# A causal mask in two attention stages: from TensorE's scores to VectorE's maxima

## The chip, the cores and the metric

The kernel runs on one core of one Trainium2 chip. Its time is the device time of one execution in microseconds. Three runs of the kernel before gave a median of 2519.93 us (2519.81 to 2523.47).

## The reference

A network of eight layers on X of shape 16 x 256 x 128 in fp32. Each layer adds its result to x. In order: differential attention, a mixture of experts with GELU, causal attention with 16 heads, the same mixture again, single-head attention, full attention with a SwiGLU mixture, a gated linear recurrence, and the attention and mixture before it once more. Two of the attentions are causal. The second of them, cut to what matters (`L0_attn_b`, per sequence of 256 positions, 16 heads of width 8):

```python
scores = jnp.einsum('bhcd,bhsd->bhcs', qi, k) * scale
mask = kpos[None, :] <= qpos[:, None]
scores = jnp.where(mask, scores, jnp.finfo(scores.dtype).min)
p = jax.nn.softmax(scores, axis=-1)
return (None, jnp.einsum('bhcs,bhsd->bhcd', p, v))
```

The differential attention (`L0_attn_a`) has 8 heads with two score maps of width 16 each, masked in the same way; its output is the first map's minus a weighted second map's, normed over 32 channels.

## The kernel before

The program is a row of stages with barriers between them. One function, `attention_stage`, makes four of them. Stage A1 (`kind` "diff") runs from about 16 to 428 us of the profile, stage A2 ("causal") from about 680 to 995 us; for both `masked` is true. A4 and A5 ("full") are not masked. Between them lie the expert stages (F1 to F4), the single-head stage A3 and the recurrence RR.

The code of each engine is written out by hand and runs in order; the engines meet at semaphores. In a masked stage the work goes in steps `n`. A step is four score maps (a quad) of one sequence, so there are `NQ` = 4 steps for each of 16 sequences. Each step has two halves `h`, each with two maps, `k` = 0, 1 (called `j` on VectorE). Scores are computed twice: once as queries x keys, only to find each query's maximum, and once turned, keys x queries, for the exponential. The kernel before does for each half:

- TensorE, `scores` (L1693): waits for `s_free` (VectorE has read the scores of the half before) and `t_free`, then `mask(k)` for both maps (L1675): a bf16 matmul of an identity (`identb`) with a mask tile (`maskS`, -1e30 above the diagonal, else 0) writes the mask into columns 0:128 and 256:384 of the map's bank. Then `score` (L1681) adds the scores on top. Query tile 0 needs keys 0:128 and lies in columns 0:128 of the map, query tile 1 needs keys 0:256 and lies in columns 128:384, so its diagonal block is columns 256:384. In between and behind, `score_t` (L1689) computes the turned scores of the step two before into `tbank`.
- VectorE, `top` (L1432): a `reduce_max` over [2 maps x 128] for query tile 0 (L1439) and one over [2 maps x 256] for tile 1 (L1440) into `padm`, then `s_free`.
- ScalarE, `exp` (L1254), into `Pm`. GpSimd, `causal` (L1133): an affine select clears what lies above the diagonal in `Pm`. That is a mask of its own, over the turned scores.

For each step TensorE also runs `weigh` (L1716, waits for GpSimd's select), `turn_max` (L1731, turns the maxima of the next step), `turn_back` (L1724) and a share of the projections of the sequence two ahead. VectorE adds the turned maxima into the queries (`with_max`, L1450) and does the statistics, norms, the division by the sums, the difference (A1), and the routing for the next expert stage (L140 to L221), each at a fixed place between two maxima. A stage has 66 steps of `top`, that is 132 halves; the two masked stages have 264. In A1 the operations L1454 to L1478 form a chain with GpSimd (`head_root`, L1091 to L1095), which gives `rr` for L1478. In A2 `dense_low` (L1401) waits for ScalarE's `high` (L1231). GpSimd also issues `send` (L225), the indirect DMAs of the routed rows, between its selects.

GpSimd builds the fp32 mask `mf` in `Pm[0]` at the start of a stage; VectorE casts it into `maskS` and the identity into `identb` (L1422, L1423).

Of the kernel before, what the change touches and what calls it, by code (L numbers as in the profile page):

```python
# [7 lines left out]
BF16 = mybir.dt.bfloat16  # L8
I32 = mybir.dt.int32
U32 = mybir.dt.uint32  # L10
ALU = mybir.AluOpType
ACT = mybir.ActivationFunctionType
AX = mybir.AxisListType.X

P = 128
D = 128
SEQ = 256
# [32 lines left out]
class Stage:  # L50
# [6 lines left out]
    def sb(self, name, shape, dt=F32):  # L57
        return self.ctx.enter_context(self.nc.sbuf_tensor(name, shape, dt))
# [4 lines left out]
    def sem(self, name):  # L63
        s = self.nc.alloc_semaphore(name)
        self.sems.append(s)
        return s
# [807 lines left out]
def attention_stage(nc, tag, kind, G, w):  # L874

    X, Y, ident = G["X"], G.get("Y"), G["ident"]
    diff, full, masked = kind == "diff", kind == "full", kind != "full"
# [10 lines left out]
    PW = 384 if masked else 512  # L888
# [52 lines left out]
    insc, outsc = sb("insc", [P, 1]), sb("outsc", [P, 1])  # L941
    if masked:
        mf = Pm[0][:, :, :].rearrange("p j k -> p (j k)")[:, 0:2 * P].rearrange("p (c k) -> p c k", k=P)
        identb, maskS = sb("identb", [P, P], BF16), sb("maskS", [P, 2, P], BF16)
    sbank, tbank = st.bank(f"{tag}_s", 2), st.bank(f"{tag}_t", 2)
    shared = [st.bank(f"{tag}_misc{k}") for k in range(2)]
    mbank, obank = st.bank(f"{tag}_mt"), st.bank(f"{tag}_ot")
# [46 lines left out]
    NEND = offset(NP, 0)  # L994
    assert NM % 2 == NMR % 2
    tail_bank = [shared[NEND % 2], shared[(NEND + 1) % 2]]
    dense_high = sem("dense_high")

    if diff:
        RSLOT = {(0, 0, 0): ("first_max", "first_gaps"), (0, 0, 1): ("first_ranks", "first_lowest", "first_choice", "others"),  # L1000
# [30 lines left out]
    with st.block() as block:  # L1031
# [334 lines left out]
        def _(dve):  # L1366
# [3 lines left out]
            def stat(b):  # L1370
                if full and b > 2:
                    dve.wait_ge(xhat_ready, b)
                for t in range(TPS):
                    last = dve.bn_stats(stats[:, t, :], XS[:, b + S0, t, :])
                last.then_inc(stat_step, 1)
                dve.wait_ge(stat_step, b + 1)
                dve.memset(spare[:, :], 0.0)
                for t in range(TPS):
                    last = dve.bn_aggr(mv[:, t, :], stats[:, t, :])
                last.then_inc(mv_ready, 1)  # L1380
# [38 lines left out]
            if split:  # L1419
                dense_low(lead["D"], 0, lead_bank["D"])  # L1420
            if masked:
                dve.tensor_copy(identb[:, :], ident[:, :])  # L1422
                dve.tensor_copy(maskS[:, :, :], mf[:, 0:2, :])  # L1423
            for k in range(2):
                dve.memset(V[k][:, :, :, DV:VG], 0.0)
            dve.memset(V[1][:, :, :, 0:DV], 0.0).then_inc(v_step, 1)
# [5 lines left out]
            def top(n, h, r, lead_in=False):  # L1432
                dve.wait_ge(s_psum, n * 2 + h + 1)
                if h == 0 and not lead_in:
                    dve.wait_ge(mt_full, n - 1)
                tops = padm[r][:, :, 2 * h:2 * h + 2, MROW]
                if masked:
                    two = sbank[:, :].rearrange("p (j k) -> p j k", j=2)
                    dve.reduce_max(tops[:, 0, :], two[:, :, 0:P], AX)  # L1439
                    last = dve.reduce_max(tops[:, 1, :], two[:, :, P:PW], AX)  # L1440
                else:
                    last = dve.reduce_max(tops.rearrange("p t j -> p j t"),  # L1442
                                          sbank[:, :].rearrange("p (j t k) -> p j t k", j=2, t=TPS), AX)
                last.then_inc(s_free, 1)
# [70 lines left out]

            dve.wait_ge(misc_full, lead["T"] + 1)
            stat(1)
            for n in range(2):
                for h in range(2):
                    top(n, h, n, lead_in=True)  # L1520
                    if (n, h) == (0, 0):
                        norm(1)
                        if full:
                            norm2(1)
# [104 lines left out]
        def _(pe):  # L1629
# [41 lines left out]
                    last = pe.matmul(misc[:, t * VW:(t + 1) * VW], xT[:, t * P:(t + 1) * P], wv[:, :], start=True, stop=True)  # L1671
                last.then_inc(misc_full, 1)

            def mask(k):
                pe.matmul(sbank[:, k * 512:k * 512 + PW].rearrange("p (c k) -> p c k", k=P)[:, 0::2, :], identb[:, :], maskS[:, :, :], start=True, stop=True)  # L1675

            def score(h, g, q, t):
                c, nk, o = g * SEQ, P if masked and t == 0 else SEQ, P if masked and t else t * SEQ
                for k in range(2):
                    r = slice((2 * h + k) * GR, (2 * h + k + 1) * GR)  # L1680
                    last = pe.matmul(sbank[:, k * 512 + o:k * 512 + o + nk], QS[q][r, c + t * P:c + (t + 1) * P], KS[q][r, c:c + nk],  # L1681
                                     start=not masked, stop=True, skip_group_check=masked)
                return last

            def score_t(h, g, q, t):
# [7 lines left out]
            def scores(n, h, g, q, first=False):  # L1693
                pe.wait_ge(s_free, n * 2 + h + 1)
                if not first:
                    pe.wait_ge(t_free, (n - 2) * 2 + h + 1)
                    if h == 0:
                        pe.wait_ge(mt_read, n)
                if masked:
                    for k in range(2):  # L1700
                        mask(k)
                gs, qs = (g, q) if first else ((g + 2) % NQ, q if g < 2 else 1 - q)
                score(h, gs, qs, 0)
                if not first:
                    score_t(h, g, q, 0)
                score(h, gs, qs, 1).then_inc(s_psum, 1)
                if not first:
                    score_t(h, g, q, 1).then_inc(t_psum, 1)
# [862 lines left out]
```

## Time and profile before

| | us |
|---|---|
| median of three runs | 2519.93 |
| span of the profiled execution | 2522.1 |
| stage A1, about | 16 to 428 |
| stage A2, about | 680 to 995 |
| TensorE busy, whole span | 2226.5 (88%) |
| VectorE busy, whole span | 1726.6 (68%) |

The profiled execution is one more execution of the same program; its span is all that the profile shows of its own time, and it is 2.2 us (0.1%) above the median. The hardware profiler gives each instruction's start and duration. "PEld" is TensorE's weight load, which overlaps the matmuls. A duration covers an instruction from start to finish; the next one on the engine can begin before that, so durations in sequence can add up to more than the busy time. A busy TensorE is not TensorE at its peak.

### The profile page before, as it was taken

The numbers are of one execution on the slowest core, as the hardware profiler recorded it, in microseconds if no ns is written. First come the engines' busy times: TensorE is split into PE (matmuls) and PEld (weight loads), VectorE is DVE, ScalarE is ACT, GpSimd is POOL, SyncE is SP. The second block draws the span as 40 slices with busy tenths as digits, with TensorE's granted clock in tenths as the row PEclk, the third lists the DMA queues.
The fourth block names the chain that finished last, engine by engine and source line by source line (L and its number), as shares of the span: only waits on it lengthen the run. The fifth ranks groups of instructions, "written<-read, shape, count | busy, mean of one in ns | idle before, by whom it ended". The sixth has DMA issues, their size and how long they took to land. (4 is left out here: it accounts for less than half of the span.)

```text
span 2522.1 us, 59734 instructions
## 1 busy us (share of the span) xinstructions
PE 2226.5 (88%) x19192; PEld 1631.9 (65%) x19192; DVE 1726.6 (68%) x4756; ACT 1597.0 (63%) x3564; POOL 1213.1 (48%) x1722
## 2 busy tenths in 40 slices
PE   8999998899699887999779888899698788888996
PEld 5666665699466655799666555589444455555795
DVE  6677776444578786544667888666788577886666
ACT  5666665377466665577548888544476178886444
POOL 4456665455244555455123566456411234665563
PEclk9999999899799999999879999899897989998998
DMA  8100000322300001222200000223300000001225
GB/s 284 63 6 12 13 12 11 102 67 71 80 2 6 16 15 53 79 70 64 71 5 2 9 17 18 71 67 82 97 1 1 5 2 4 17 17 55 67 79 138
DMA packets 134005, 116.57 MB, mean 46 GB/s; under 512 B 22919, under 2 KB 120213, under 8 KB 131664
## 3 DMA queue, kind: packets, MB, share of 16 engines
q1 hardware_dynamic: 116432, 78.17, 11.0%
q0 software_dynamic: 17280, 34.65, 4.2%
q8 instruction: 164, 2.69, 0.5%
q14 instruction: 129, 1.06, 0.1%
HBM read 58.22 MB, written 56.36 MB: 45 GB/s over the span
## 5 line engine op out<-in xcount | busy, mean ns | idle before, releaser
L1254 ACT ACTIVATE A_Pm<-A_t 128x768 f32<-128x768 f32 (+1 forms) x512 | 468.6, 915 | 157.6 <-PE A_t L1689 153.5
L371 POOL DMA_INDIRECT ybuf<-F_yo,F_idx x284 | 315.7, 1112 | 248.9 <-DVE F_yo L580 146.0
L1442 DVE TENSOR_REDUCE A_padm<-A_s 128x4 f32<-128x1024 f32 x264 | 322.7, 1222 | 66.1 <-PE A_s L1681 64.7
L225 POOL DMA_INDIRECT xbuf<-xs,dst x256 | 270.0, 1055 | 104.0 <-issue 58.4
L741 PE MATMUL F_hb<-F_xT,F_wt 128*128 128x128 f32 x2272 | 305.9, 278 | 1.0 <-issue 0.6
L1716 PE MATMUL A_ot<-A_Pm,A_V 128*32 128x256 f32 (+3 forms) x3640 | 296.8, 390 | 11.0 <-POOL A_Pm L1133 10.0
L1689 PE MATMUL A_t<-A_Q,A_K 32*128 32x256 f32 (+1 forms) x2560 | 305.9, 333 | 0.0
L1133 POOL TENSOR_SCALAR_AFFINE_SELECT A_Pm<-A_Pm 128x512 f32<-128x512 f32 x256 | 167.7, 655 | 285.6 <-ACT A_Pm L1254 284.0
L741 PEld LDWEIGHTS F_hb<-F_xT,F_wt 128*128 128x128 f32 x2272 | 275.6, 192 | 7.2 <-issue 2.4
L1681 PE MATMUL A_s<-A_K,A_Q 32*128 32x256 f32 (+1 forms) x1584 | 202.1, 332 | 60.0 <-DVE A_padm L1442 42.1
L753 PE MATMUL F_out<-F_WA,F_g 128*128 x1704 | 244.9, 280 | 6.1 <-DVE F_g L571 3.0
L753 PEld LDWEIGHTS F_out<-F_WA,F_g 128*128 128x128 f32 x1704 | 212.8, 191 | 8.9 <-issue 7.6
L1681 PEld LDWEIGHTS A_s<-A_K,A_Q 32*128 32x128 f32 x1584 | 122.8, 188 | 145.8 <-DVE A_padm L1442 72.0
L590 DVE COPY F_wt<-F_WA 128x644 f32 (+1 forms) x284 | 131.0, 462 | 122.7 <-DVE F_yo L580 72.7
L1689 PEld LDWEIGHTS A_t<-A_Q,A_K 32*128 32x128 f32 x2560 | 203.4, 185 | 6.3
L1716 PEld LDWEIGHTS A_ot<-A_Pm,A_V 128*32 128x32 f32 (+1 forms) x3640 | 114.4, 114 | 122.0 <-issue 50.1
L427 ACT ACTIVATE F_g<-F_hb,F_wt 128x128 f32<-128x128 f32 x568 | 162.1, 368 | 32.9 <-PE F_hb L741 32.8
L1440 DVE TENSOR_REDUCE A_padm<-A_s 128x2 f32<-128x512 f32 x264 | 180.5, 684 | 0.0
L1439 DVE TENSOR_REDUCE A_padm<-A_s 128x2 f32<-128x256 f32 x264 | 112.8, 427 | 85.0 <-PE A_s L1681 83.8
L1258 ACT ACTIVATE A_OT<-A_ot 128x256 f32<-128x256 f32 (+1 forms) x260 | 113.9, 438 | 81.7 <-PE A_ot L1716 81.7
L1724 PE MATMUL A_ot<-ident,A_OT 128*128 128x128 f32 x650 | 128.9, 297 | 2.2 <-ACT A_OT L1258 2.2
L1450 DVE TENSOR_TENSOR A_Q<-A_Q,A_mt 128x256 fp32r<-128x256 f32 (+1 forms) x260 | 108.3, 416 | 31.2 <-PE A_mt L1731 20.0
(424 smaller groups left out, 4938.6 us busy)
## 6 DMA issues: line engine op xcount, KB each, us to landing
F_xr<-xbuf SPq DMA_DIRECT2D x284, 68.0 KB, 1.9
xbuf<-A_zero SPq DMA_DIRECT2D x16, 1088.0 KB, 18.0
xs<-ybuf SPq DMA_DIRECT2D x32, 512.0 KB, 7.0
ybuf<-F_yo,F_idx POOLq DMA_INDIRECT x284, 2.5
xbuf<-xs,dst POOLq DMA_INDIRECT x256, 2.6
F_WA<-in_L_ffn_ew SPq DMA_DIRECT2D x2, 2048.0 KB, 9.2
F_WA<-in_L_ffn_ew SPq DMA_DIRECT2D x16, 256.0 KB, 5.6
F_WA<-in_L_ffn_e_gate SPq DMA_DIRECT2D x2, 1024.0 KB, 5.8
```

The costliest lines, as they stand in the source:

```text
L225: pool.indirect_dma_start(out=G["XBUF"][:, :], out_offset=bass.IndirectOffsetOnAxis(ap=G["dst"][:, t, c:c + 1], axis=0), in_=G["xs"][c][:, ...
L371: pool.indirect_dma_start(out=YBUF[:, :], out_offset=bass.IndirectOffsetOnAxis(ap=idx[n][:, h:h + 1], axis=0), in_=yo[r][:, h, :], in_offs ...
L427: last = act.activation(g[q][:, c, :], hb[2 * q + c // 2][:, c % 2 * TILE:(c % 2 + 1) * TILE], ACT.Gelu_apprx_tanh, bias=b1[r][:, c:c + 1])
L741: pe.matmul(hb[2 * q + c // 2][:, c % 2 * TILE:(c % 2 + 1) * TILE], w1[r][:, c * P:(c + 1) * P], xT[q][:, 0:TILE], start=True, stop=True). ...
L753: last = pe.matmul(outb[:, h * D:(h + 1) * D], g[q][:, c, h * P:(h + 1) * P], w2[:, bass.ds(e, 1), c, :].rearrange("p a d -> p (a d)"), st ...
L1133: pool.affine_select(out=keep, in_=keep, compare_op=ALU.is_ge, fill=0.0, base=0, pattern=[[0, 2], [0, 2], [1, P]], channel_multiplier=-1). ...
L1254: act.activation(Pm[r][:, j:j + 2, :], tbank[:, :].rearrange("p (j k) -> p j k", j=2)[:, :, 0:PW], ACT.Exp, scale=SCALE).then_inc(t_free, 1)
L1440: last = dve.reduce_max(tops[:, 1, :], two[:, :, P:PW], AX)
L1442: last = dve.reduce_max(tops.rearrange("p t j -> p j t"), sbank[:, :].rearrange("p (j t k) -> p j t k", j=2, t=TPS), AX)
L1681: last = pe.matmul(sbank[:, k * 512 + o:k * 512 + o + nk], QS[q][r, c + t * P:c + (t + 1) * P], KS[q][r, c:c + nk], start=not masked, stop ...
L1689: last = pe.matmul(tbank[:, k * 512 + keys(t).start:k * 512 + keys(t).stop], K1[q][r, c + t * P:c + (t + 1) * P], Q2[g % 2][r, q0:SEQ], st ...
L1716: last = pe.matmul(obank[h * VG:(h + 1) * VG, 0:NS * SEQ].rearrange("p (s q) -> p s q", s=NS)[:, :, q0:], V[q][:, s, g * QUAD // NS + h, : ...
```

## The change

The mask is no longer put into PSUM by TensorE. `score` writes plain scores, and `top` adds the mask while it takes the maximum: one `tensor_tensor_reduce` for each map and each query tile, four for a half (two over 128 elements, two over 256). Each reads the scores out of PSUM and an fp32 mask row `mask3` ([128 x 384]: the diagonal block's mask, zeros, the mask again) out of SBUF, writes the sum as bf16 into a tile `masked_s` that nothing reads, and gives the maximum as a second output into `padm`. `identb`, `maskS`, `mask` and its calls are gone. At the start of a stage two casts become a clearing and two copies, with a semaphore `mask_set` that VectorE itself waits for ahead of the first maximum. GpSimd's select on `Pm` stays.

```diff
     if masked:
-        identb, maskS = sb("identb", [P, P], BF16), sb("maskS", [P, 2, P], BF16)
+        mask3, masked_s = sb("mask3", [P, 3 * P]), [sb(f"masked_s{k}", [P, 2, 2, PW], BF16) for k in range(2)]
...
-    dense_high = sem("dense_high")
+    dense_high, mask_set = sem("dense_high"), sem("mask_set")
...
             if masked:
-                dve.tensor_copy(identb[:, :], ident[:, :])
-                dve.tensor_copy(maskS[:, :, :], mf[:, 0:2, :])
+                dve.memset(mask3[:, P:2 * P], 0.0)
+                for c in (0, 2):
+                    last = dve.tensor_copy(mask3[:, c * P:(c + 1) * P], mf[:, 0, :])
+                last.then_inc(mask_set, 1)
...
                 tops = padm[r][:, :, 2 * h:2 * h + 2, MROW]
                 if masked:
-                    two = sbank[:, :].rearrange("p (j k) -> p j k", j=2)
-                    dve.reduce_max(tops[:, 0, :], two[:, :, 0:P], AX)
-                    last = dve.reduce_max(tops[:, 1, :], two[:, :, P:PW], AX)
+                    for j in range(2):
+                        for t, (c, width) in enumerate(((0, P), (P, SEQ))):
+                            last = dve.tensor_tensor_reduce(masked_s[r][:, h, j, c:c + width], sbank[:, j * 512 + c:j * 512 + c + width], mask3[:, c:c + width],
+                                                            1.0, -3e38, ALU.add, ALU.max, tops[:, t, j:j + 1])
...
             stat(1)
+            if masked:
+                dve.wait_ge(mask_set, 1)
...
-            def mask(k):
-                pe.matmul(sbank[:, k * 512:k * 512 + PW].rearrange("p (c k) -> p c k", k=P)[:, 0::2, :], identb[:, :], maskS[:, :, :], start=True, stop=True)
-
             def score(h, g, q, t):
...
-                                     start=not masked, stop=True, skip_group_check=masked)
+                                     start=True, stop=True)
...
-                if masked:
-                    for k in range(2):
-                        mask(k)
                 gs, qs = (g, q) if first else ((g + 2) % NQ, q if g < 2 else 1 - q)
                 score(h, gs, qs, 0)
```

## Rows read from the trace of the kernel before

**Rows 1.** The page: span, and busy time of each engine.
```profile
span 2522.1 us, 59734 instructions
...
PE 2226.5 (88%) x19192; PEld 1631.9 (65%) x19192; DVE 1726.6 (68%) x4756; ACT 1597.0 (63%) x3564; POOL 1213.1 (48%) x1722
```

**Rows 2.** Busy time by stretch: inside A1, then inside A2.
```profile
core 0: us, PE busy (x) PEld busy (x) DVE busy (x) ACT busy (x) POOL busy (x), PEclk, DMA share, GB/s
100.00:400.00 300.00, 300.00 (x2484) 199.13 (x2484) 225.15 (x623) 197.86 (x389) 178.92 (x228) 1.00 0.03 10
750.00:950.00 200.00, 177.57 (x2107) 120.89 (x2107) 161.41 (x518) 135.85 (x275) 106.88 (x168) 1.00 0.04 12
```

**Rows 3.** Groups by line, VectorE, 100 to 400 us: the first maximum.
```profile
L1439 DVE TENSOR_REDUCE A_padm<-A_s 128x2 f32<-128x256 f32 x94 | 39.8, 424 | 31.0 <-PE A_s L1681 30.5
```

**Rows 4.** The same, 750 to 950 us.
```profile
L1440 DVE TENSOR_REDUCE A_padm<-A_s 128x2 f32<-128x512 f32 x85 | 58.0, 682 | 0.0
L1439 DVE TENSOR_REDUCE A_padm<-A_s 128x2 f32<-128x256 f32 x85 | 35.9, 422 | 13.7 <-PE A_s L1681 13.3
```

**Rows 5.** Timeline of TensorE in A2: start, duration, instructions.
```profile
838.12 0.38 PE L1675 MATMUL A_s<-A_maskS,A_identb 128*128 128x256 bf16 x2
838.43 0.33 PE L1681 MATMUL A_s<-A_K,A_Q 32*128 32x128 f32 x2
```

**Rows 6.** Waits over 16 to 428 us (A1): total, times, longest.
```profile
DVE A_padm L1439 <- PE A_s L1681: 52.4, 91, 2.6
...
DVE A_ctx L1478 <- POOL A_rr L1095: 25.5, 16, 1.6
DVE X L1490 <- ACT A_Q L1224: 21.2, 15, 2.0
...
PEld A_s L1675 <- DVE A_padm L1440: 1.7, 3, 0.8
```

**Rows 7.** Waits over 698 to 995 us (A2).
```profile
PEld A_s L1675 <- DVE A_padm L1440: 27.1, 51, 1.0
...
DVE A_low L1401 <- ACT A_high L1231: 14.0, 16, 1.0
PEld A_ot L1716 <- POOL A_Pm L1133: 13.8, 20, 1.2
```

**Rows 8.** Timeline of VectorE in A2, one maximum and what follows.
```profile
819.62 0.42 DVE L1439 TENSOR_REDUCE A_padm<-A_s 128x2 f32<-128x256 f32 x1
819.95 0.68 DVE L1440 TENSOR_REDUCE A_padm<-A_s 128x2 f32<-128x512 f32 x1
820.54 0.41 DVE L1450 TENSOR_TENSOR A_Q<-A_Q,A_mt 128x256 fp32r<-128x256 f32 x1
820.87 0.15 DVE L175 TENSOR_TENSOR d<-A_r 128x4 f32<-128x4 f32 x1
...
821.54 0.43 DVE L1439 TENSOR_REDUCE A_padm<-A_s 128x2 f32<-128x256 f32 x1 [0.35 <-PE A_s L1681]
```

**Rows 9.** Groups by line, whole span: two-operand adds and multiplies out of PSUM.
```profile
L1450 DVE TENSOR_TENSOR A_Q<-A_Q,A_mt 128x256 fp32r<-128x256 f32 x195 | 81.4, 418 | 31.2 <-PE A_mt L1731 20.0
...
L580 DVE TENSOR_TENSOR F_yo<-F_out,F_wt 128x128 f32<-128x128 f32 x142 | 41.4, 291 | 77.0 <-PE F_out L753 76.7
```

**Rows 10.** Timeline of ScalarE: operations that also give a sum.
```profile
1324.74 0.30 ACT L1300 ACTIVATE A_squares_next<-Y 128x128 f32<-128x128 f32 x1
1324.94 0.19 ACT L1300 ACTIVATION_READ_ACCUMULATOR A_squares_next<-Y 128x1 f32 x1
1325.03 0.30 ACT L1300 ACTIVATE A_squares_next<-Y 128x128 f32<-128x128 f32 x1
```

**Rows 11.** Timeline of VectorE: seven clearings of one element.
```profile
5.59 0.23 DVE L1368 MEMSET A_credit<- 128x1 f32 x7 [0.41 <-PEq L813]
```

**Rows 12.** Timeline of VectorE, a multiply beside GpSimd work in A1.
```profile
261.95 1.64 DVE L1460 TENSOR_TENSOR A_T<-A_O,A_rec 128x1024 f32<-128x1024 f32 x1
```

**Rows 13.** The same multiply at the end of A1, GpSimd idle.
```profile
434.83 1.22 DVE L1460 TENSOR_TENSOR A_T<-A_O,A_rec 128x1024 f32<-128x1024 f32 x1
```

## The prediction

> **What bounds the kernel now.** I read the page first: TensorE is busy for 88% of the span and VectorE for 68% [rows 1]. That is an average over ten stages, and the change touches only two of them, so the next view is the busy time by stretch. The reader should see two different cases there. Inside A1 TensorE is busy all the time, VectorE for 225 of 300 us. Inside A2 TensorE leaves a gap (178 of 200 us) and VectorE is busy for 161 us [rows 2]. The groups by line give the number of maxima in these stretches, 94 and 85 [rows 3, 4]. One half of a step, which holds one maximum, therefore takes 300 / 94 = 3.19 us in A1 and 200 / 85 = 2.35 us in A2. VectorE is busy for 225.15 / 94 = 2.40 us and 161.41 / 85 = 1.90 us of that. TensorE needs 3.19 and 2.09 us.
>
> The waits say who holds whom. In A1 TensorE hardly ever waits for a maximum (3 times), while VectorE waits 91 times for scores [rows 6]: TensorE is the bound. In A2 TensorE waits for a maximum in 51 of 132 halves, 27.1 us together, and 20 times for GpSimd's select [rows 7]. There the loop of scores, maximum, scores is already closed in a good part of the halves, and VectorE sits in it.
>
> **What is removed.** In each half TensorE no longer issues the two mask matmuls. Their cost is not their duration of 0.38 us but the step from their start to the first score: 838.43 - 838.12 = 0.31 us [rows 5]. For 132 halves that is 41 us of TensorE in each stage, and for A1, if nothing else came in, 41 us of time. The loop gains too: from the end of one maximum (820.63) to the start of the next (821.54) pass 0.91 us now [rows 8], and 0.60 us without the masks.
>
> **What is added.** Today a maximum takes from 819.62 to 819.95 + 0.68 = 820.63, so 1.01 us [rows 8]. After the change four operations stand there, two over 128 and two over 256 elements, each with two operands, one out of PSUM. The trace has no such operation that also gives a maximum, so I cost it in two parts.
>
> The pass over the elements: the nearest rows are the two-operand operations out of PSUM, 291 ns for 128 and 418 ns for 256 elements, so 127 ns for 128 elements more [rows 9]. On the engine's path an operation counts by its step: 820.54 to 820.87 is 0.33 us for 256 elements [rows 8], hence 0.33 - 0.13 = 0.20 us for 128. Two of each are 1.06 us, and the last one ends 0.09 us after its step (0.418 - 0.33): 1.15 us, 0.14 us more than today. The whole of that comes from paying the fixed part four times in place of two.
>
> Giving out the maximum: the nearest rows are ScalarE's operations that also give a sum. The profile shows a second instruction for it, which starts 0.20 us after its operation, and the next operation starts another 0.09 us later [rows 10]. The lower end is VectorE's own smallest work that only writes, seven one-element clearings in 0.23 us, 0.03 us each [rows 11]. I take 0.07 us, nearer to the read-out, because it is the same kind of work, and below it, because ScalarE's fixed parts are longer throughout. Four times 0.07 is 0.28 us. The Trainium skill (VectorE: DVE Perf Modes, "Two Vector instructions with no wait between them") says of this engine too that an operation that also writes out its accumulator is two instructions. No row of this trace shows it on VectorE. By that rule the 0.28 us are due; were the maximum given for nothing, the sum below would be 54 us faster than before and not 20 us slower.
>
> So a maximum becomes longer by x = 0.14 + 0.28 = 0.42 us, from 1.01 to 1.43.
>
> **The sum by stage.** VectorE's new half is its busy time, plus x, plus the idle time that stays.
> A1: idle time is 3.19 - 2.40 = 0.79 us a half. 52.4 / 132 = 0.40 of that is waiting for scores [rows 6] and goes, since TensorE would now need only 3.19 - 0.31 = 2.88. The waits for GpSimd's `rr` (25.5 / 132 = 0.19) and for ScalarE's copy ahead of `add_y` (21.2 / 132 = 0.16) [rows 6] lie on chains of their own and stay: 0.35. The new half is 2.40 + 0.42 + 0.35 = 3.17 us against 3.19, so -3 us over 132 halves. The bound moves from TensorE to VectorE and the gain is eaten.
> A2: idle time is 0.45 us. The wait for scores, 13.3 / 85 = 0.16 [rows 4], shrinks. The wait for `high` is 14.0 / 132 = 0.11 [rows 7] and stays, and I leave 0.09 for halves in which VectorE has less than 0.60 us of other work to fill the loop: 0.20. The new half is 1.90 + 0.42 + 0.20 = 2.52 us against 2.35, so +0.17, or +22 us.
> Together +20 us, worked out against the profiled execution of 2522.1 us [rows 1]; the median lies 2.2 us lower, and 2519.9 + 20 is 2540 us. In general the change is 132 x (2x - 0.69) = 264x - 91 us. It is zero at x = 0.345, a read-out of 0.051 us.
>
> **Edits at nothing.** At each stage's start two casts become a clearing and two copies, all ahead of the first maximum, for which VectorE waits for scores anyway (part of the wait of up to 2.6 us in [rows 6]); uncovered, they would cost some 0.3 us a stage. The wait on `mask_set` is for work done long before. GpSimd's select and `send` are unchanged. What is queued behind a longer maximum is `with_max` and the routing steps; for `with_max` waits `score_t` of the next step, for the routing GpSimd's sends. They have a whole half of slack.
>
> **The rivals.**
> *The read-out is cheap (faster).* At 0.03 us, as the clearings, x is 0.27 and the change -20 us; at nothing, x is 0.14: -54 us. It decides below 0.051 us. For it speaks that the clearings run on the same engine; against it, that the one read-out in the trace takes three times as long. Times 2466 to 2505, 2500 most likely. Chance 0.24.
> *The operations do not overlap.* If each must end before its read-out, and that before the next, a maximum takes 2 x (0.291 + 0.418) + 4 x 0.09 = 1.78 us and x is 0.77. Waits then shrink further, say by 0.15 in A1 and 0.10 in A2: 132 x (2.40 + 0.77 + 0.20 - 3.19 + 1.90 + 0.77 + 0.10 - 2.35) = +79 us, 2599. Against it: today's maxima do overlap by 0.09 us [rows 8]. The Trainium skill (VectorE: DVE Perf Modes, "The DRAIN you can't avoid") says that the next operation does not start until the pipe is empty; by that, this case would hold, while [rows 8] show an operation starting before the one ahead has ended. Into the same case falls contention with GpSimd, which stretches a multiply with both operands in SBUF from 1.22 to 1.64 us [rows 12, 13]. The new operations have one there; L1450, which has that too, shows 0.41 alike [rows 8, 9]. Chance 0.10.
> *The loop absorbs it (no change).* If outside the 51 halves that now wait for a maximum [rows 7] other chains (GpSimd's select, the projections) hold A2, only those grow, by x - 0.31 = 0.11 us, +6 us, and A1 stays at -3: 2523. Chance 0.12.
>
> **How the numbers follow.** The forecast case (a read-out of 0.05 to 0.10 us, 2522 to 2565) has 0.54. Slower by over 0.2% (5 us, about what a measurement of this kernel can tell from no change) gets the forecast's 0.52, 0.10 of the case without overlap: 0.62. Faster gets 0.24. The rest, 0.14, lies within 0.2%. The range reaches from a read-out a little below the clearings' price, 2490, to the case without overlap, 2600.
>
> **What would show it.** Right: the four operations of a maximum take 1.35 to 1.5 us from start to end, with a read-out each; TensorE in A1 falls below 95% busy and VectorE rises above 85%; A1 keeps its length within 10 us, A2 grows by 15 to 30 us; TensorE's waits for VectorE's maxima appear in A1. Wrong: a maximum below 1.3 us, with A1 shorter by 15 us or more, or a half of A2 that stays at 2.35 us although VectorE's maximum is longer.

## The result and the profile after

The changed kernel takes 2507.61 us (median of 4 runs, 2506.87 to 2508.09) against 2521.47 for the kernel before beside it: ratio 0.9941, 95% interval [0.9928, 0.9955]. It is faster by 0.6%, 14 us, where 20 us slower was forecast. The profiled execution has a span of 2506.1 us.

The same views as before the change, now of the changed kernel. The page:

```profile
span 2506.1 us, 60276 instructions
...
PE 2180.2 (87%) x18664; PEld 1610.6 (64%) x18664; DVE 1758.4 (70%) x6342; ACT 1595.4 (64%) x3564; POOL 1209.4 (48%) x1722
```

TensorE has lost 46 us of busy time and VectorE has gained 32 [rows 1]. One maximum on VectorE, from its timeline (start, duration, instruction):

```profile
830.07 0.29 DVE L1442 CUSTOM_DVE_ANT_0 A_masked_s<-A_s,A_mask 128x128 bf16<-128x128 f32 x1
830.28 0.08 DVE L1442 DVE_READ_ACCUMULATOR2_ANT A_padm<- 128x1 f32 x1
830.28 0.42 DVE L1442 CUSTOM_DVE_ANT_0 A_masked_s<-A_s,A_mask 128x256 bf16<-128x256 f32 x1
830.62 0.09 DVE L1442 DVE_READ_ACCUMULATOR2_ANT A_padm<- 128x1 f32 x1
830.62 0.29 DVE L1442 CUSTOM_DVE_ANT_0 A_masked_s<-A_s,A_mask 128x128 bf16<-128x128 f32 x1
830.84 0.08 DVE L1442 DVE_READ_ACCUMULATOR2_ANT A_padm<- 128x1 f32 x1
830.84 0.42 DVE L1442 CUSTOM_DVE_ANT_0 A_masked_s<-A_s,A_mask 128x256 bf16<-128x256 f32 x1
831.18 0.08 DVE L1442 DVE_READ_ACCUMULATOR2_ANT A_padm<- 128x1 f32 x1
831.18 0.29 DVE L1374 BATCH_NORM_STATS2 A_stats<-X 128x6 f32<-128x128 f32 x1
```

This is the view that decides the case. There is a read-out, and it has its own row of 0.08 us. But each one starts at the same moment as the next operation (830.28, 830.62, 830.84, 831.18): it lies beside it and adds nothing to the step. The steps are 0.21 us for 128 and 0.34 for 256 elements, and a maximum takes 831.18 + 0.08 - 830.07 = 1.19 us. With today's 1.01 [rows 8], x is 0.18 and not 0.42.

Stage lengths in the two profiles, from VectorE's first instruction of a stage to its first of the next (A1 from the start of the execution):

| us | before | after | |
|---|---|---|---|
| A1 | 449.7 | 429.9 | -19.8 |
| the stage between A1 and A2 | 217.7 | 219.8 | +2.1 |
| A2 | 332.7 | 342.4 | +9.7 |
| all that follows | 1522.0 | 1514.0 | -8.0 |

A1 gains and A2 loses. No instruction of the last row was changed. Half of it (394.3 to 390.1 us) lies in one stretch between the full stages, F3 and the recurrence, whose length scatters from 388.7 to 394.3 us over the kernels of this study on chips of this speed. The two masked stages alone are worth -10 us in these profiles; the rest of the 14 us of the median I can't assign.

Busy time by stretch (start:end, then length, PE, PEld, DVE, ACT, POOL, granted TensorE clock, DMA share, GB/s). To compare, each stretch starts equally far behind the start of its stage in both kernels. Before:

```profile
690.00:970.00 280.00, 250.92 (x2954) 170.00 (x2955) 220.58 (x693) 188.38 (x379) 143.07 (x230) 0.99 0.03 10
30.00:430.00 400.00, 400.00 (x3303) 265.54 (x3303) 294.95 (x796) 264.36 (x517) 232.10 (x297) 1.00 0.13 53
```

After:

```profile
672.00:952.00 280.00, 233.07 (x2657) 163.25 (x2657) 232.00 (x1371) 180.77 (x369) 136.28 (x224) 0.93 0.03 10
30.00:410.00 380.00, 366.11 (x3032) 244.61 (x3031) 305.27 (x1554) 263.28 (x516) 228.84 (x297) 1.00 0.14 56
```

and the read-outs in the same two stretches after, four to a half:

```profile
L1442 DVE DVE_READ_ACCUMULATOR2_ANT A_padm<- 128x1 f32 x464 | 38.3, 83 | 0.0
...
L1442 DVE DVE_READ_ACCUMULATOR2_ANT A_padm<- 128x1 f32 x506 | 41.6, 82 | 0.0
```

That makes 116 halves in A2's stretch (119 before) and 126.5 in A1's (127 before), and with them a half:

| us a half | length | TensorE busy | VectorE busy |
|---|---|---|---|
| A1 before | 3.15 | 3.15 | 2.32 |
| A1 after | 3.00 | 2.89 | 2.41 |
| A2 before | 2.35 | 2.11 | 1.85 |
| A2 after | 2.41 | 2.01 | 2.00 |

Two things are to be seen. In A1 TensorE is still busy for 96% of the time: it stays the bound, and the half is 0.11 us above what TensorE needs. Its busy time fell by 0.26 us a half, at a clock of 1.00, so the masks were worth a little less than the 0.31 of their step. In A2 TensorE lost two mask matmuls that stood for 0.31 us, but is busy for only 0.10 us less: its granted clock has fallen from 0.99 to 0.93. A stretch of TensorE's timeline in A2 shows what that is:

```profile
833.30 1.51 PE L1715 MATMUL A_ot<-A_Pm,A_V 128*32 128x256 f32 x16 [1.48 <-POOL A_Pm L1133]
834.73 0.69 PE L1730 MATMUL A_mt<-ident,A_padm 128*128 128x128 f32 x2
...
837.84 1.91 PE L1650 MATMUL A_misc<-A_xT,A_raw 128*128 128x256 f32 x4
```

and the granted clock over the last of these instructions:

```profile
837.80:839.70 1.90, 1.90 (x10) 1.07 (x8) 0.45 (x3) 0.00 (x0) 0.38 (x1) 0.50 0.00 0
```

TensorE stood idle for 1.48 us for GpSimd's select, and the work behind it ran at a granted clock of 0.50, the lower of its two levels (1.2 GHz). In the middle of A2 the clock falls to that level nine times in this profile, for 41 us together, each time behind gaps of TensorE whose longest is 0.75 to 1.49 us. In the kernel before it stays at 1.00 from 697 to 996 us, and the longest gap in the middle of the stage is 1.02 us. Before the change the same four matmuls, here too, take 1.03 us, in a stretch with a granted clock of 1.00 throughout [rows 2]:

```profile
837.26 1.03 PE L1645 MATMUL A_misc<-A_xT,A_raw 128*128 128x256 f32 x4
```

Waits over 16 to 420 us (A1), after:

```profile
DVE A_ctx L1481 <- POOL A_rr L1095: 31.7, 16, 2.1
...
DVE X L1493 <- ACT A_Q L1224: 21.3, 16, 1.9
DVE A_masked_s L1442 <- PE A_s L1683: 17.5, 38, 2.5
PEld A_ot L1715 <- POOL A_Pm L1133: 16.9, 16, 1.3
...
PEld A_s L1683 <- DVE A_padm L1442: 13.5, 33, 0.9
```

and over 700 to 980 us (A2):

```profile
PEld A_s L1683 <- DVE A_padm L1442: 40.4, 68, 1.3
...
PEld A_ot L1715 <- POOL A_Pm L1133: 21.1, 19, 1.7
PE A_s L1683 <- DVE A_padm L1442: 19.5, 40, 1.0
```

VectorE's wait for scores in A1 falls from 52.4 to 17.5 us, and does not vanish [rows 6]. TensorE now waits for maxima in A1 too (33 times against 3), and in A2 more than before [rows 7].

### The profile page after: what moved, and what is told of

It reads as the page before. It is cut to its first block and busy times, and to the rows that moved or that the text cites. A ratio compares the mean times of both kernels' runs of the same rounds, so it can differ in the third digit from the quotient of the medians.

```text
span 2506.1 us, 60276 instructions
## 1 busy us (share of the span) xinstructions
PE 2180.2 (87%) x18664; PEld 1610.6 (64%) x18664; DVE 1758.4 (70%) x6342; ACT 1595.4 (64%) x3564; POOL 1209.4 (48%) x1722
## 5 line engine op out<-in xcount | busy, mean ns | idle before, releaser
L1442 DVE CUSTOM_DVE_ANT_0 A_masked_s<-A_s,A_mask 128x128 bf16<-128x128 f32 (+1 forms) x1056 | 313.8, 355 | 34.6 <-PE A_s L1683 32.7
L1683 PEld LDWEIGHTS A_s<-A_K,A_Q 32*128 32x128 f32 x1584 | 126.5, 192 | 182.1 <-DVE A_padm L1445 71.0
L418 ACT ACTIVATE F_xT<-F_xt,swiglu_nw 128x128 f32<-128x128 f32 x142 | 52.2, 368 | 108.6 <-PE F_xt L731 108.6
```

Source lines behind the costliest of these rows:

```text
L1442: last = dve.tensor_tensor_reduce(masked_s[r][:, h, j, c:c + width], sbank[:, j * 512 + c:j * 512 + c + width], mask3[:, c:c + width], 1.0 ...
```

## The experiments

Three theories stood after the result. **The read-out**: it costs no step, x is 0.18, and that alone turns the sign. **The masks**: what TensorE gains has nothing to do with x, and the forecast had its 0.31 us wrong. **The idle time**: the forecast's formula has the waits that stay too small, since with x = 0.18 it gives 264 x 0.18 - 91 = -43 us and -14 were measured.

The kernels ran on several chips of unlike speed (the kernel before took 2580.45, 2522.5, 2562.64 and 2523.61 us in the four groups below), so each is compared with the kernel before in its own group. On the slower chips the stages that no kernel touches were longer; A1 and A2 of the kernel before, or of a kernel that leaves one of them as it was, agreed within 1.5 us everywhere, and are compared across groups. Each length is read from one profiled execution. For the changed A2 four profiles give 341.1 to 344.6 us, and for A2 without any mask two give 330.8 and 327.6, so a difference of 3 us in A2 says little.

### One stage at a time

The first, `a1_only`, changes A1 alone; `a2_only` has the two kinds the other way round:

```diff
+    TTR, PEM = kind in ("diff",), kind in ("causal",)
-                if masked:
+                if TTR:
                     for j in range(2):
...
+                if PEM:
+                    for k in range(2):
+                        mask(k)
```

> VectorE masks its maxima in A1 alone; A2 is the kernel before's, with TensorE's mask matmuls. In the profile of the changed kernel A1 is 19.8 us shorter (start of the run to the first norm of F1: 449.7 to 429.9 us) and A2 9.7 us longer (332.7 to 342.4 us, from the stage's first clearing to F2's first norm). If the two stages do not touch each other, this kernel gets the whole gain and none of the loss: A1 -19 to -20 us, A2 within 2 us of before, the time about 2501 us, 18 to 22 us faster than before. The rival is that the two are tied (semaphores, clock, or the place of the code): then A2 moves here too, or A1 gives less.

Measured: 2561.35 us, ratio 0.9932 [0.9916, 0.9948]. A1 takes 432.1 us, 17.6 less than before and not the 19 to 20 expected; A2 is as before.

> VectorE masks its maxima in A2 alone; A1 is the kernel before's. If the stages are independent: A1 as before (449.7 us), A2 about 342 us, the time 8 to 12 us above before, some 2531 us, with TensorE's granted clock below 1.00 in parts of A2 as in the changed kernel. If A2's growth came from where A1 left things (the clock, the sends' places), A2 stays near 333 us and the time near before's.

Measured: 2586.82 us, ratio 1.0026 [1.0016, 1.0037]. A2 takes 342.1 us, where `a1_only` beside it has 333.2 with A2 as it was before.

So the change is a gain of 0.7% in A1 and a loss of 0.3% in A2. The forecast's formula at x = 0.18 gives -34 us for A1 and -9 us for A2: too much gain in the one, the wrong sign in the other.

### No mask at all, and no maximum given out

`no_mask` leaves the mask out of the maxima: neither TensorE nor VectorE adds it.

```diff
-                            last = dve.tensor_tensor_reduce(...)
+                two = sbank[:, :].rearrange("p (j k) -> p j k", j=2)
+                dve.reduce_max(tops[:, 0, :], two[:, :, 0:P], AX)
+                last = dve.reduce_max(tops[:, 1, :], two[:, :, P:PW], AX)
```

> Left out: any mask in the scores from which the maxima are taken. No mask matmuls and no adding on VectorE; the maxima are the two plain reductions of before, over all keys that are in the bank. The softmax itself keeps GpSimd's select. So TensorE is as light as in the changed kernel and a maximum takes 1.01 us as before, not 1.19. Theory one (the longer maximum is what makes A2 longer): A2 falls below before's 332.7 us, to about 320 us, and A1 falls below 429.9 - to about 420 us - since a maximum is 0.18 us shorter in 132 halves each: the time 2475 to 2490 us. Theory two (A2 is longer because TensorE, with less to do, gets a lower clock in parts of it): the clock falls here too and A2 stays at 333 to 342 us.

Measured: 2549.3 us, ratio 0.988 [0.9865, 0.9895]. A1 428.6, A2 330.8 us, with the granted clock in the middle of A2 at 0.93.

`no_read` keeps the four passes and gives no maximum out:

```diff
-                            last = dve.tensor_tensor_reduce(masked_s..., sbank..., mask3..., 1.0, -3e38, ALU.add, ALU.max, tops[:, t, j:j + 1])
+                            last = dve.tensor_tensor(masked_s..., sbank..., mask3..., ALU.add)
```

> Left out: the maxima. Each of the four operations of a half is a plain two-operand add of the mask (scores out of PSUM, mask out of SBUF, bf16 result), so there is no second instruction that reads the maximum out; the column for the maximum stays zero. If the read-outs cost nothing, as the steps of 0.21 and 0.34 us in the changed kernel's trace say, the time is that of the changed kernel within 5 us (2503 to 2510 us) and A1 and A2 keep their lengths within 3 us each. If each costs the 0.07 us of the prediction, 1056 of them are worth 74 us of VectorE and the time falls by 20 us or more below the changed kernel's.

Measured: 2568.81 us, ratio 0.9962 [0.9948, 0.9975]. A1 429.6, A2 339.7 us, against 429.9 and 342.4 with the read-outs. Its timeline has the four additions in one row, and what follows them:

```profile
829.47 1.15 DVE L1454 TENSOR_TENSOR A_masked_s<-A_s,A_mask 128x128 bf16<-128x128 f32 x4
830.54 0.48 DVE L1378 BATCH_NORM_STATS2 A_stats<-X 128x6 f32<-128x128 f32 x2
```

Four plain additions take a step of 830.54 - 829.47 = 1.07 us, and the four with a maximum 831.18 - 830.07 = 1.11. All that the maxima cost is 0.01 us each, where the forecast had 0.07. Without them the stages are shorter by 0.3 and 2.7 us. The read-out theory holds.

`no_mask` shows the other side. Its maximum is as short as before and TensorE has no masks, the best that both could give, and yet A2 stands at 330.8 us, 2 us below the kernel before. Neither of the expectation's theories has this length (about 320, or 333 to 342 us); the lower clock of the second is there. In A1, 428.6 us is only 1.3 below the changed kernel. There the maximum no longer decides.

### The changed kernel again

The first of the second group, the changed kernel as it is:

> The changed kernel as it is, once more on the chip of the runs beside it. Its ratio to before was 0.9941 [0.9928, 0.9955] on the first chip. Expected 0.993 to 0.996 here, A1 429 to 432 us and A2 341 to 344 us. If the two single-stage kernels (0.9932 and 1.0026) add up, 0.9932 + 0.0026 = 0.9958.

Measured: 2511.22 us, ratio 0.9968 [0.995, 0.9986]; A1 430.3, A2 341.1 us. The stages are where they were. With the first comparison the gain is between 0.3 and 0.6%, faster in both.

### Masks on TensorE again, with the new maximum

`both_masks` computes VectorE's masked maxima and lets TensorE issue its mask matmuls as before (their product is overwritten by the scores).

```diff
+                for k in range(2):
+                    mask(k)
                 gs, qs = (g, q) if first else ((g + 2) % NQ, q if g < 2 else 1 - q)
```

> TensorE does its two mask matmuls in each half as before (the scores then overwrite them), and VectorE masks again while it takes the maxima, as in the changed kernel. So TensorE's work is that of before, and a maximum is 0.18 us longer: this takes the longer maximum alone. If the longer maximum is the price, A2 is 8 to 15 us longer than before (341 to 348 us) at a granted clock of 1.00, and A1 0 to 6 us longer (449 to 456), since TensorE bounds it: the time 1.003 to 1.009 of before. If the lower clock is the price, A2 stays within 4 us of before's 333 us, because TensorE stays busy.

Measured: 2538.49 us, ratio 1.0068 [1.0051, 1.0085]. A1 453.7 us (+4.0 against before), A2 345.3 us (+12.6), clock 1.00 in both:

```profile
100.00:400.00 300.00, 298.24 (x2462) 197.43 (x2459) 233.93 (x1185) 196.33 (x386) 170.90 (x224) 1.00 0.03 10
750.00:950.00 200.00, 175.67 (x2042) 117.46 (x2042) 169.17 (x987) 132.61 (x268) 98.91 (x160) 1.00 0.04 11
```

This splits the change in two. In A1 the longer maximum costs 4 us and the masks' removal gives 24 of the 41 that TensorE had for them. In A2 the longer maximum costs 12.6 us and the removal gives 3 to 4. That is the surprise: a step of 0.31 us is gone from a loop in which TensorE waits, and next to nothing comes back.

### A longer maximum: the forecast's own x

`longer_max` adds to each maximum a further addition over 163 elements, whose step is 0.24 us, so that a maximum takes the 1.43 us which the forecast had given it.

```diff
+                    last = dve.tensor_tensor(extra[:, :], sbank[:, 0:163], mask3[:, 0:163], ALU.add)
```

> The changed kernel with one more two-operand add of 163 elements on VectorE behind the four of each half, into a tile that nothing reads: about 0.24 us more per maximum (0.07 us of fixed step and 0.17 us of elements). That puts the maximum at 1.43 us, what the prediction had assumed with a read-out of 0.07 us. If the prediction's sum was right but for the read-out, this kernel is 20 us slower than before: 1.008. If also the idle time that it let stay was wrong, by the changed kernel's slope (A2 11 us longer for 0.18 us, A1 1 us), then A2 grows by another 15 us to about 357 us, A1 by 2 to 15 us to 432 to 445 us, and the ratio to before is 1.001 to 1.006.

Measured: 2541.94 us, ratio 1.008 [1.0063, 1.0097]. A1 442.5 us (-7.2 against before; the forecast had -3), A2 359.8 us (+27.1; the forecast had +22). Its timeline:

```profile
829.32 0.28 DVE L1455 CUSTOM_DVE_ANT_0 A_masked_s<-A_s,A_mask 128x128 bf16<-128x128 f32 x1
...
830.42 0.32 DVE L1457 TENSOR_TENSOR A_extra<-A_s,A_mask 128x163 bf16<-128x163 f32 x1
830.66 0.41 DVE L1467 TENSOR_TENSOR A_Q<-A_Q,A_mt 128x256 fp32r<-128x256 f32 x1
```

The added step is 830.66 - 830.42 = 0.24 us. With the price that the forecast had for the maximum, the kernel is slower by 0.8%, 19 us above the 2522.5 of before beside it; the forecast had +20. One number, the read-out, carried the sign. That the size agrees as well is in part luck, as the section on the masks' removal shows.

### What holds A1 at 430 us

`no_rr` takes VectorE's longest remaining wait in A1 away: GpSimd writes its powers `rr` aside and VectorE multiplies by ones. The kernel leaves out the norm of A1, whose factor is not 1, as the expectation has it: its output is not the network's, and only the length of A1 is read from it.

```diff
-                pool.tensor_tensor(rr[:, :], sm2[:, :], ...).then_inc(rr_ready, 1)
+                pool.tensor_tensor(rr_aside[:, :], sm2[:, :], ...).then_inc(rr_ready, 1)
-                    dve.wait_ge(rr_ready, k + 1)
```

> The changed kernel, but in A1 VectorE does not wait for GpSimd's reciprocal roots ahead of the normed context (a wait of 31.7 us in A1); GpSimd computes them all the same, into another tile. Left out: the norm over a head's channels, whose factor is 1 here. If this chain (sums, three GpSimd operations, context, next maximum) keeps A1 at 430 us where TensorE's work would allow less, A1 falls to 405 to 420 us and the time by 10 to 25 us below the changed kernel's. If A1 is held elsewhere (GpSimd's select ahead of the weighing, ScalarE's copies), A1 stays within 4 us of 430.

Measured: 2508.79 us, ratio 0.994 [0.9923, 0.9956]; A1 426.7 us, 3.6 below the changed kernel beside it, though a wait of 31.7 us was gone. VectorE's wait for scores took its place, over the same 16 to 420 us. Between 100 and 400 us nothing moved: TensorE is busy for 289.1 us in both kernels, with 2399 matmuls against 2398 in the changed one. The line of that wait:

```profile
DVE A_masked_s L1457 <- PE A_s L1700: 51.1, 54, 2.8
```

`short_select` cuts GpSimd's zeroing of weights to eight columns, in both stages. Most weights of later keys stay in, so the kernel leaves out the causal mask; it is there for its time alone.

```diff
-                keep = Pm[r][:, j:j + 2, 0:2 * P]
+                keep = Pm[r][:, j:j + 1, 0:8]
```

> The changed kernel with GpSimd's zeroing of the weights of later keys cut from 128x512 (0.64 us) to 128x8 elements in both masked stages, so that most weights of later keys are left in. It asks what holds the first masked stage at 427 to 430 us, where neither the last 0.18 us of the maximum nor the wait for GpSimd's power moves it. If the chain of one half (exponential on ScalarE, zeroing on GpSimd, weighting on TensorE) holds it, some 0.5 us of each of 128 halves goes, or of each of 64 quads where one half's zeroing lies beside the other's exponential: the first stage falls by 20 to 60 us. If TensorE's or VectorE's own work holds it, it falls by less than 8 us. In the second stage the same: 20 us or more against less than 8.

Measured: 2525.38 us, ratio 0.9858 [0.9838, 0.9878]. A1 423.2 us (-7), A2 327.6 us (-14 against the changed kernel's 341.1 to 342.4). Busy time of its middle of A1:

```profile
100.00:400.00 300.00, 296.08 (x2458) 198.07 (x2457) 241.45 (x1277) 212.63 (x419) 136.00 (x247) 1.00 0.03 11
```

In A1 neither `rr`, nor a shorter maximum, nor the select gives back more than 7 us. TensorE is busy for 96% of the middle of A1 in the changed kernel and in `no_rr`, 97% in `no_mask` and 99% here. TensorE's own work is the bound of A1 after the change, with 0.11 us a half lost to the other engines together. In A2 the select is worth 14 us of 342, between the two cases of the expectation (20 or more, less than 8). TensorE's longest idle time there falls from 1.49 to 1.02 us, but most of the 14 us come through the clock, as the next section shows.

### Where the masks' removal went in A2

Two causes were left: the granted clock, which falls to 0.93 when the masks are gone, ate it; or the loop of scores and maxima had slack. The first attempt filled TensorE with matmuls that nobody reads, in A2 alone, twice a quad (`fill_a2` on the changed kernel, `no_mask_fill` on the one without masks):

```diff
             def weigh(n, g, q):
...
+                if kind == "causal":
+                    for k in range(3):
+                        pe.matmul(obank[:, 256:384], G["C"]["ones"][:, :], G["C"]["before"][:, :], start=True, stop=True)
```

> The changed kernel, and in the second masked stage alone TensorE gets three further 128x128 bf16 matmuls at the head of each weighting and of each turning back of the output; their product goes into a free part of the output's bank and is never read. No other work changes. The question is whether the granted clock of 0.91 to 0.93, which the second masked stage shows since TensorE's mask matmuls are gone, eats what their removal should have given. If it does, the clock goes back to 1.00 and the stage shortens from about 342 us towards 332 us (2,500 us in all). If TensorE's speed is not what the stage waits for, the clock may rise, but the stage stays at 340 to 345 us (2,507 us). If the fillers stand on the path, the stage grows by up to 64 x 6 x 0.06 us x 2, some 30 us at most.

Measured: 2552.3 us, ratio 0.9967 [0.9949, 0.9985]; A2 342.2 us, clock 0.97 over 750 to 950 us where the changed kernel has 0.91. (The product in the expectation is 46 us, not 30.)

> No mask in the maxima at all (two plain reductions of 128 and 256 columns each half, neither TensorE's mask nor VectorE's; the scores of later keys then count in the maximum), with the same three filler matmuls twice a quad in the second masked stage. Against the kernel without mask and without fillers it asks the question of the clock again, at a cheap maximum: if the clock (0.93 there) holds the stage, it goes from 331 us to below 325 us; if not, 328 to 336 us.

Measured: 2539.37 us, ratio 0.9916 [0.9888, 0.9944]; A2 337.7 us, clock 0.95.

> No mask in the maxima at all, as before on another chip (0.988 there), now beside the fillers. Both theories: 0.985 to 0.991, first masked stage 428 to 431 us, second 329 to 333 us at a granted clock of 0.93.

Measured: 2535.15 us, ratio 0.9898 [0.9879, 0.9918]; A1 427.6, A2 327.6 us, clock 0.93.

This did not tell the two apart. The fillers bring a step of 0.46 us a quad with them (0.28 ahead of the weighting, 0.18 ahead of the turning back), up to 29 us in a stage, and the clock rose only part of the way. On the changed kernel price and gain may cancel; on the one without masks the fillers cost 7 to 10 us by the profiles. The profiled execution of `no_mask_fill`, 2551 us, is the slowest of its five; by the medians the two kernels differ by 0.2%, within their intervals.

The second attempt left the clock alone. A second mask pair was added to kernels that have one and a clock of 1.00 (`both_masks` and the kernel before), in A2:

```diff
-                    for k in range(2):
+                    for k in (0, 1, 0, 1) if kind == "causal" else (0, 1):
                         mask(k)
```

> The kernel that has both TensorE's masks and VectorE's four masked maxima (345.3 us in the second masked stage, granted clock 1.00), with TensorE's mask pair issued twice there: 0.31 us more of TensorE in each of 132 halves, at a clock that stays at 1.00. Taking the first pair away gave only 3 to 4 us (341 to 342 us), and the clock fell to 0.91 with it. If the falling clock ate the rest of that gain, a second pair at full clock costs what the loop of scores and maxima says, 0.31 us in those halves (a half to all of them) in which the loop is closed: 355 to 385 us. If the stage hardly waits for this loop, it costs as little as the first pair gave: 346 to 351 us.

Measured: 2554.63 us, ratio 1.0129 [1.0103, 1.0154]; A2 360.3 us, 15.0 above `both_masks`.

> The kernel before (332.7 and 333.2 us in the second masked stage, clock 1.00), with the mask pair issued twice there. The same question with the short maximum of 1.01 us, where TensorE is busy for 178 of 200 us: if the removal of the pair gave only 2 to 5 us because the clock fell, the second pair costs 15 to 41 us (348 to 374 us); if the loop has slack, below 8 us (up to 341 us).

Measured: 2542.9 us, ratio 1.0084 [1.0056, 1.0112]; A2 350.5 us, 17.8 above the kernel before. The clock stays at 1.00. The first of the two, TensorE's timeline and the middle of A2:

```profile
838.21 0.60 PE L1692 MATMUL A_s<-A_maskS,A_identb 128*128 128x256 bf16 x4
838.74 0.33 PE L1698 MATMUL A_s<-A_K,A_Q 32*128 32x128 f32 x2
```

```profile
750.00:950.00 200.00, 183.85 (x2106) 127.76 (x2104) 162.55 (x934) 125.98 (x255) 92.67 (x150) 1.00 0.03 11
```

Two pairs are a step of 0.53 us where one is 0.31, so the second pair puts 0.22 us into a half, 29 us into the stage, and 15 to 18 of them, 52 to 61%, show in its length. The first pair is 41 us; by that share its removal should have given 21 to 25. It gave 3 to 4 with the new maximum, and 2 to 5 with the old one (`no_mask` against before). The difference between adding at full clock and taking away with a falling one is some 17 to 23 us, and the granted clock is what differs.

That could still be a loop that bends just there, with slack below one pair and none above it. The trace of the changed kernel itself settles it, because parts of its A2 run at full clock. The same place of the program, behind the same wait of 1.48 us, is there twice, once at 1.00 and once (above, from 833.30) at 0.50:

```profile
793.57 0.86 PE L1715 MATMUL A_ot<-A_Pm,A_V 128*32 128x256 f32 x16 [1.48 <-POOL A_Pm L1133]
...
796.10 1.03 PE L1650 MATMUL A_misc<-A_xT,A_raw 128*128 128x256 f32 x4
797.30 0.33 PE L1683 MATMUL A_s<-A_K,A_Q 32*128 32x128 f32 x2 [0.17 <-issue]
...
839.68 0.44 PE L1683 MATMUL A_s<-A_K,A_Q 32*128 32x128 f32 x2
```

From the weighting to the scores of the next half pass 797.30 - 793.57 = 3.73 us at full clock and 839.68 - 833.30 = 6.38 at the lower level: 2.65 us more in a stretch of 6.8. The middle of A2 is at the lower level for 41 us, so I estimate from this pair that the clock costs it some 16 us. The starts of all maxima say the same. The program repeats every 16 halves (two sequences), and each of the 102 halves from the 21st on can be compared with the halves at the same place that ran wholly at full clock, as did the one ahead of them. "Touched" are all the others:

| A2, us | a half at full clock | halves touched by the lower level | what these took more |
|---|---|---|---|
| before | 2.37 | 0 | 0 |
| `both_masks` | 2.45 | 0 | 0 |
| changed kernel, two profiles | 2.28, 2.20 | 23, 26 | 16, 23 |
| no mask, two profiles | 2.20, 2.20 | 19, 19 | 14, 14 |
| `fill_a2` | 2.38 | 6 | 6 |
| `no_mask_fill` | 2.28 | 17 | 13 |
| `short_select` | 2.25 | 9 | 6 |
| `longer_max` | 2.36 | 30 | 22 |

At full clock the masks' removal does shorten the half, by 0.17 to 0.25 us with the new maximum and by 0.17 with the old one, 22 us or more over the stage: about the share that the second pair shows. The halves at the lower level take 14 to 23 us of it back. So the clock is the cause, and the loop does not bend. `fill_a2` is explained too (0.10 us or more a half for the fillers, 10 us or more won from the clock), as is `no_mask_fill` (0.08 us a half for the fillers, 1 us won), and `short_select` (its half at full clock is within the two of the changed kernel; it loses less to the clock). What stays open is what makes the clock fall just where it does: the wait of 1.48 us that ended at 793.57 was not followed by a fall, the one that ended at 833.30 was.

## Why the prediction was wrong, point by point

**The step that failed** is the term "four times 0.07 is 0.28 us" for giving out the maximum. It measured 0.01 us each by the steps of `no_read` and the changed kernel, 0.04 in all, so x was 0.18 and not 0.42. The forecast knew the lower bound and named its break-even of 0.051 us; it chose between the bounds by likeness of kind, from ScalarE's read-out [rows 10], where the next operation starts behind the read-out's start. On VectorE it starts together with it. The reason for going below ScalarE's price, fixed parts that are longer throughout, had no row: by rows of the kernel before, copies out of PSUM take 277 and 385 ns for 128 and 256 elements on ScalarE, where VectorE's operations take 291 and 418, so I estimate a fixed part of some 0.17 and 0.16 us. The Trainium skill (VectorE: DVE Perf Modes, "Two Vector instructions with no wait between them") was right that there are two instructions; it says nothing of what the second costs, and the prediction read a price into it ("by that rule the 0.28 us are due"). Two rows are not two steps.

**The passes over the elements** were right: 1.15 us forecast, 1.15 measured for the four plain additions of `no_read` and 1.19 with the maxima in it; durations 286 and 419 ns against the 291 and 418 of [rows 9].

**The idle time that stays** was the second error, on the other side, and it hid part of the first. By the forecast's sum at x = 0.18 A1 has a half of 2.40 + 0.18 + 0.35 = 2.93 us, above the 2.88 that TensorE was to need. Over the forecast's own stretch, 100 to 400 us, there are now 394 read-outs, 98.5 halves: the half is 3.05, TensorE needs 2.94 (289.2 / 98.5; the masks gave 0.25 and not 0.31), VectorE is busy for 2.49 (245.0 / 98.5) and idle for 0.56, not 0.35. So the half fell by 0.14 us where the formula at x = 0.18 has 0.26, 20 us over the stage where it has 34. The bound did not move to VectorE, which is busy for 80% and not above 85%, while TensorE stays at 96%.

**A2** grew, as forecast, but by 8 to 10 us and not 22, and with the right x the formula has the wrong sign: 1.90 + 0.18 + 0.20 = 2.28 us a half, -9 us. That 2.28 is what the halves at full clock take (2.20 and 2.28). The 18 us between are the price of the granted clock, which the forecast took as unchanged: 16 and 23 us in the two profiles. With it the idle time is 0.41 us and not 0.20; 0.09 of that 0.20 had no row.

**At its own x the forecast's total came out, in part by luck**: `longer_max` gave -7 and +27 us where -3 and +22 were forecast. In A1 TensorE is busy for 94% there and VectorE for 85%, so VectorE is not the only bound, as the formula has it. In A2 VectorE is busy for 87%, TensorE for 81%, and the clock is at 0.89 (750 to 950 us): at full clock a half takes 2.36 us, as before the change and not 2.52, and the lower level adds 22 us that the formula does not have. From x = 0.42 to 0.18 A1 gained 12 us and A2 18 where 32 each were due, and from 0.18 to none, 1 to 3 us and 10 to 15.

**One bound of a case** does not fit its own formula: read-outs of 0.05 and 0.10 us give 2519 and 2571 us, not 2522 and 2565. Nothing hangs on it.

**The rivals.** *The read-out is cheap* was the case that came, just above its times (2466 to 2505), by the idle time. *The operations do not overlap* is refuted by the timeline: steps of 0.21 and 0.34 us under durations of 0.29 and 0.42. The Trainium skill (VectorE: DVE Perf Modes, "The DRAIN you can't avoid") has the next operation wait for an empty pipe, and says in the same paragraph that one which is not held starts earlier. The prediction gave only the first half. These rows agree with the second: the next operation starts 0.08 us before the one ahead has ended. Contention with GpSimd did not show in the new operations either: 286 and 419 ns in both stages. *The loop absorbs it* did not come: A2 grew by more than its 6 us, and A1 did not stay.

**Of what was to be seen**, the list for "wrong" came true nearly to the letter: a maximum below 1.3 us and A1 shorter by over 15. TensorE's waits for maxima in A1 did appear.

**The better kernel** of this study is the one that adds no mask to the maxima at all, 0.988 and 0.9898 of the time before. A maximum that also counts later keys is never below the one that is wanted, and the weights of later keys are zeroed by GpSimd in any case; what it gives up is precision where a later key's score is far above all that count; that is argued, and no run measures how much. Changing A1 alone gives 0.9932, no worse than the whole change (0.9941 and 0.9968).

## What to carry to other kernels

When a new instruction has a second row in the profile, ask where the next operation starts, not how long the row is; a term whose bounds lie on both sides of break-even leaves the sign open, and a guess by likeness does not close it. Taking work from an engine that is at its limit gives less than its time when the next engine is nearly as full: here 0.11 us a half was left between TensorE's busy time and the half. Taking cheap matmuls from TensorE in a stage where it already waits can cost it the clock. Add a second copy of the work to learn what the first is worth at full clock, and compare the same place of the program at both levels within one trace. A total that comes out at the assumed price is no proof of the terms: read the clock of each stage first.

## What the runs showed of the hardware

- VectorE's read-out of a maximum: a row of 82 ns that starts together with the next operation; 0.01 us more to the step than a plain addition of the same shape.
- TensorE's granted clock fell to 0.50 (1.2 GHz) behind an idle time of 1.48 us in A2, and four 128x256 matmuls took 1.91 us in place of 1.03. The Trainium skill (TensorE: Matmul & The Clock Gate, "Part 1: The HAM clock gate") ties the lower level to an engine that has been idle. The trace agrees in that each fall in A2 came behind gaps, but they were short ones in a stage in which TensorE was busy for 83%, and one wait of 1.48 us had no fall behind it.
- With the two bf16 mask matmuls in each half the clock stayed at 1.00 from 697 to 996 us, all of A2 but its first 30 and last 4 us; without them it fell nine times in the middle of the stage.
- Two more bf16 mask matmuls of 256 columns behind the first two cost a step of 0.22 us, the first two 0.31.
